# Scores a slot later, spreads at the slot's end, and two VectorE pairs merged, in a windowed-attention stack

## What is computed

```python
x = attn_layer(shift_tokens(x)) + x
x = ffn_layer(shift_tokens(x)) + x

def attn_layer(x):                       # 16 heads of 64
    q, k, v = split(x @ Wqkv)
    q, k = l2norm(q) * qs, l2norm(k) * ksc
    q = q * cos * scale + rotate_half(q) * sin * scale
    k = k * cos / scale + rotate_half(k) * sin / scale
    # local attention: windows of 32; a query sees itself and the 32 keys before it
    sim = where(mask, -max, 8 * q @ k.T)
    return softmax(sim) @ v @ Wo

def ffn_layer(x):
    a, gate = split(layernorm(x) @ W1 + b1)   # 2 x 341
    return a * gelu(gate) @ W2 + b2
```

## Time and profile before

| | before |
|---|---|
| median of 3 runs | 4340.56 us |
| profiled execution | 4352.9 us |
| its span, first to last instruction | 4351.2 us |
| TensorE busy | 4027.8 us (93%) |
| VectorE busy | 3345.6 us (77%) |
| ScalarE busy | 3100.0 us (71%) |
| GpSimd busy | 1798.7 us (41%) |
| mean granted TensorE clock | 0.959 of full speed |

### The profile page before, as it was taken

The page is one execution under the profiler, slowest core; times in us unless marked ns, Lnnn a source line. Parts: engine busy times, 40 slices in busy tenths (PEclk is TensorE's granted clock), DMA queues, the critical chain, the costliest instruction groups (busy, mean ns, idle before and its releaser), DMA issues. The chain is left out here.

```text
span 4351.2 us, 113662 instructions
## 1 busy us (share of the span) xinstructions
PE 4027.8 (93%) x43857; PEld 2388.8 (55%) x43857; DVE 3345.6 (77%) x4981; ACT 3100.0 (71%) x7032; POOL 1798.7 (41%) x1071
## 2 busy tenths in 40 slices
PE   7997999999999999999967689999999999999998
PEld 3443555555555555555536545555555555555554
DVE  5774888888888888888735478888888888888885
ACT  3555777777777777777762267777777778777776
POOL 3111444444444444444404534444444444444442
PEclk7997999999999999999986589999999999999999
DMA  2212444444443443444300044444434444444342
GB/s 44 31 21 70 95 111 102 99 101 101 105 111 90 111 107 90 111 99 103 84 10 3 3 107 109 101 97 109 110 87 115 102 100 100 102 105 111 92 100 52
DMA packets 232520, 380.78 MB, mean 88 GB/s; under 512 B 59364, under 2 KB 122336, under 8 KB 231688
## 3 DMA queue, kind: packets, MB, share of 16 engines
q1 hardware_dynamic: 231560, 372.20, 36.9%
q10 hardware_dynamic: 384, 0.79, 0.1%
HBM read 39.22 MB, written 1.05 MB: 9 GB/s over the span
## 5 line engine op out<-in xcount | busy, mean ns | idle before, releaser
L835 POOL TENSOR_TENSOR b_prob<-b_prob,b_rinv 128x768 f32<-128x768 f32 x384 | 564.3, 1469 | 1778.3 <-DVE b_rinv L1281 1778.3
L841 POOL TENSOR_TENSOR b_prc<-b_prc,b_sws 128x1024 f32<-128x1024 f32 x384 | 907.7, 2364 | 72.2 <-DMA b_sws<-b_prs 72.2
L1143 ACT ACTIVATE b_prob<-ps,b_nmx 128x96 f32<-128x96 f32 x3072 | 749.0, 363 | 0.0
L885 PEld LDWEIGHTS ps<-ident,b_prob 128*128 128x128 f32 x3072 | 367.9, 140 | 406.5 <-ACT b_pT L1079 232.8
L1216 DVE SCALAR_TENSOR_TENSOR b_prc<-ps,b_qks,b_rot 128x512 f32<-128x512 f32 x768 | 571.1, 744 | 14.0 <-ACT b_sq L1104 13.3
L1218 DVE SCALAR_TENSOR_TENSOR b_prs<-ps,b_qks,b_rot 128x512 f32<-128x512 f32 x768 | 570.1, 742 | 0.0
L885 PE MATMUL ps<-ident,b_prob 128*128 128x128 f32 x3072 | 513.0, 281 | 46.5 <-DVE b_kr L1264 37.1
L1262 DVE TENSOR_TENSOR b_prc<-b_prc,ps 128x512 f32<-128x512 f32 x384 | 263.6, 686 | 369.9 <-PE ps L950 288.3
L1079 ACT ACTIVATE b_pT<-ps 128x512 f32<-128x512 f32 x724 | 435.5, 601 | 154.1 <-PE ps L885 151.1
L987 PE MATMUL ps<-b_wqkv,b_xs 128*128 128x256 f32 x1536 | 435.0, 406 | 2.2 <-DVE b_prs L1218 2.2
L938 PE MATMUL ps<-b_xs,b_wqkv 128*128 128x512 f32 x768 | 408.9, 614 | 23.3 <-issue 10.0
(11 more groups left out here) (293 smaller groups left out, 7218.0 us busy)
## 6 DMA issues: line engine op xcount, KB each, us to landing
b_sws<-b_prs SPq DMA_DIRECT2D x1536, 128.0 KB, 2.3
b_vs<-b_va SPq DMA_DIRECT2D x384, 256.0 KB, 3.8
b_wqkv<-in_L_ffn_Wqkv SPq DMA_DIRECT2D x96, 192.0 KB, 3.6
b_xs<-y SPq DMA_DIRECT2D x126, 128.0 KB, 2.3
b_wo<-in_L_ffn_Wo SPq DMA_DIRECT2D x96, 64.0 KB, 3.1
b_xs<-y SPq DMA_DIRECT2D x42, 127.8 KB, 2.4
b_rot<-in_rot SPq DMA_DIRECT2D x2, 2048.0 KB, 7.8
b_w<-in_L_ffn_W SPq DMA_DIRECT2D x24, 170.5 KB
```

The costliest lines, as they stand in the source:

```text
L835: pool.tensor_tensor(prob[:, r, :, P - KEYS:P], prob[:, r, :, P - KEYS:P], rinv[:, r % 2, :].rearrange("p (b a) -> p b a", a=1).broadcast_ ...
L841: pool.tensor_tensor(prc[:, r, :, :], prc[:, r, :, :], sws[:, r % 2, :, :], ALU.add)\
L885: t = pe.transpose(bank[6][:, i * P:(i + 1) * P], prob[:, kd, 4 * e + 2 * h + m, :], ident[:, :])
L1143: g = act.activation(prob[:, kb, i, P - KEYS:P], wide[0][:, e * CH + m * KEYS:e * CH + (m + 1) * KEYS], ACT.Exp, bias=nmx[:, kb % 2, i:i + 1])
```

## The change

On TensorE, T0 now comes right behind Q, the scores follow it and are those of `c_` (unit(3)) instead of `b` (unit(2)), then K, T1, V, the strips, U, and at the end the spreads of b, just ahead of W. The spreads go to banks 7 and 6, the strips to bank 3, U and the feed-forward to bank 2. W, which writes bank 3 as before, waits in odd slots for `ln_done`, ScalarE's reading of the strips. On ScalarE the eight exponentials (now of `c_`) stand behind the copy of T1 and ahead of the copy of the values, `oT` and the inverse norms. On VectorE the maxima come behind the q product, then the split, the k product, the sums and reciprocals, and one normalising product at the end. The cosine and the sine product of q (and of k) are one instruction over 2 x 512 elements with the bank read twice, and so are the two normalising products, which read banks 6 and 7 in one call. The copy of T0 is always ScalarE's.

```diff
 # tensor
+                def spreads(b, d, pe=pe):
+                    UB, kb = um(b)
+                    pe.wait_ge(S["split_done"], ONE + twos(b) + 1)
+                    pe.wait_ge(S["kn_done"], ONE + UB)
+                    pe.matmul(bank[7], take[:, 2 * (kb % 2) + 1, :], rsp[:, :], start=True, stop=True)
+                    if d:
+                        pe.wait_ge(S["pt_cp"], ONE + 2 * um(d)[0] + 2)
+                    pe.matmul(bank[6], take[:, 2 * (kb % 2), :], rsp[:, :], start=True, stop=True).then_inc(S["nb_mm"], 1)
...
                         pe.matmul(bank[0][:, :], W[:, 0, :], X, start=True, stop=True).then_inc(S["q_mm"], 1)
...
-                    if d and before != 5:
-                        turn(UD, kd, 0)
+                        turn(UD, kd, 0, c_)
+                    if c_:
+                        UC, kc = um(c_)
+                        if not d:
+                            scores_ready(UC)
+                        mask(kc)
...
+                        g.then_inc(S["s_mm"], 1)
                     key_bank_free(f0)
                     if a:
                         pe.wait_ge(S["pk_done"], ONE + U)
                         pe.matmul(bank[1][:, :], W[:, 1, :], X, start=True, stop=True).then_inc(S["k_mm"], 1)
-                    if d and before == 5:
-                        turn(UD, kd, 1, b)
-                    if d and before != 5:
-                        turn(UD, kd, 1, b)
-                    if a and j % 2 and before != 5:
-                        strips(U, b)
-                    if b:
-                        if not d:
-                            scores_ready(UB)
-                        mask(kb)
...
-                        g.then_inc(S["s_mm"], 1)
-                    value_bank_free(f0)
                     if d:
-                        values(d, 0)
-                        values(d, 1)
+                        turn(UD, kd, 1)
...
                         m.then_inc(S["va_mm"], 1)
-                    if a and j % 2 and before == 5:
-                        strips(U, b)
+                    if a and j % 2:
+                        strips(U, d)
+                    value_bank_free(f0)
+                    if d:
+                        values(d, 0)
+                        values(d, 1)
+                    if b:
+                        spreads(b, d)
...
                         pe.wait_ge(S["o_cp"], ONE + UD + 1)
...
                         pe.wait_ge(S["y_add"], ONE + UD)
+                        if a and j % 2:
+                            pe.wait_ge(S["ln_done"], ONE + twos(a) + 1)
                         pe.matmul(bank[3][:, :], wo[:, pair(d), :], oT[:, kd % 2, :], start=True, stop=True).then_inc(S["wo_mm"], 1)
 # scalar
-                    if a and j % 2 and before != 5:
-                        inverse_norms(twos(a))
-                    if d:
-                        act.wait_ge(S["pv_mm"], ONE + 2 * UD + 2)
-                        act.activation(oT[:, kd % 2, :], bank[7], ACT.Copy).then_inc(S["o_cp"], 1)
...
                         act.preload_act_table_set("natural_log_exp_and_others")
+                    if c_:
+                        UC, kc = um(c_)
+                        act.wait_ge(S["smax_done"], ONE + UC + 1)
...
+                        g.then_inc(S["exp_done"], 1)
                     if a:
                         act.wait_ge(S["va_mm"], ONE + U + 1)
...
+                    if step == 2:
+                        act.wait_ge(S["f_norm"], ONE + C + 1)
+                        act.activation(fin, fin, ACT.Identity, bias=lng[:, 1:2]).then_inc(S["f_in"], 1)
+                    if d:
+                        act.wait_ge(S["pv_mm"], ONE + 2 * UD + 2)
+                        act.activation(oT[:, kd % 2, :], bank[2], ACT.Copy).then_inc(S["o_cp"], 1)
+                    if a and j % 2:
                         inverse_norms(twos(a))
 # vector
-                    dve.scalar_tensor_tensor(out=prc[:, r, i, :], in0=bank[i][:, :], scalar=scale,
-                                             in1=rot[:, 2 * i, t], op0=ALU.mult, op1=ALU.mult)
-                    dve.scalar_tensor_tensor(out=prs[:, r % 2, i, :], in0=bank[i][:, :], scalar=scale,
-                                             in1=rot[:, 2 * i + 1, t], op0=ALU.mult, op1=ALU.mult).then_inc(S[done], 1)
+                    both = bank[i][:, :].rearrange("p (a c) -> p a c", a=1).broadcast_to([P, 2, CH])
+                    dve.scalar_tensor_tensor(out=two_runs((2 * r + i) * CH, (8 + 2 * (r % 2) + i) * CH), in0=both, scalar=scale,
+                                             in1=rot[:, 2 * i:2 * i + 2, t], op0=ALU.mult, op1=ALU.mult).then_inc(S[done], 1)
...
-                        dve.tensor_copy(pT[:, 0, :, :], bank[6].rearrange("p (i q) -> p i q", i=4)).then_inc(S["pt_cp"], 1)
...
-                        dve.tensor_tensor(prc[:, kb, 0, :], prc[:, kb, 0, :], bank[2][:, :], ALU.mult).then_inc(S["qn_done"], 1)
-                        at = PAD + (kb % 2) * CH
-                        dve.tensor_tensor(kr[:, at:at + CH], prc[:, kb, 1, :], bank[3][:, :], ALU.mult).then_inc(S["kn_done"], 1)
...
+                        dve.wait_ge(S["s_mm"], ONE + UC + 1)
+                        dve.tensor_reduce(nmx[:, kc % 2, :], sc, AX.X, ALU.max, negate=True).then_inc(S["smax_done"], 1)
...
+                        at = 12 * CH + PAD + (kb % 2) * CH
+                        dve.tensor_tensor(two_runs(2 * kb * CH, at), prc[:, kb, :, :], norms, ALU.mult).then_inc(S["kn_done"], 1)
```

More of the change, by code:

```diff
@@ L624, in stack_semaphores, with stack @@
     return {n: sem("b_" + n) for n in names.split()}
-def stack(rep, ln_call, S, nc, w, c, bank, wide, xT, y, ident, identb, jmean, ln_eps, ss_eps, ss_back,
+def stack(rep, ln_call, S, nc, w, c, bank, wide, xT, y, ident, identb, jmean, norms, ln_eps, ss_eps, ss_back,
           ln_pe, ln_act, ln_dve, norm_done, cs, cen, sqr):
@@ L677, in stack, with two_runs @@
         ZERO = 8
+        def two_runs(first, second):
+            return bass.AP(roll[:, :].tensor, first, [roll[:, :].ap[0], [second - first, 2], [1, CH]])
         def um(u):
@@ L906, in values @@
                                 es = slice(e * DH, (e + 1) * DH)
-                                t = pe.matmul(bank[7][es, n * BLK:(n + 1) * BLK], v[:, es],
+                                t = pe.matmul(bank[2][es, n * BLK:(n + 1) * BLK], v[:, es],
                                               pT[:, h, 2 * e + m, o * BLK:(o + 1) * BLK],
@@ L1007, in slot @@
                             pe.wait_ge(S["ffw_ld"], ONE + 208 * (L0 + f[0] + 1))
-                        pe.matmul(bank[7], w1[:, 0, i * P:(i + 1) * P], fin, start=True, stop=True).then_inc(S["f_a"], 1)
+                        pe.matmul(bank[2], w1[:, 0, i * P:(i + 1) * P], fin, start=True, stop=True).then_inc(S["f_a"], 1)
                     if ok is not None:
@@ L1011, in slot @@
                         for i in range(FT):
-                            m = pe.matmul(bank[7], w2[:, i, :], hid[:, i, :], start=(i == 0), stop=(i == FT - 1))
+                            m = pe.matmul(bank[2], w2[:, i, :], hid[:, i, :], start=(i == 0), stop=(i == FT - 1))
                         m.then_inc(S["f_out"], 1)
@@ L1080, in turned, with query_squares @@
                             .then_inc(S["pt_cp"], 1)
+                    def query_squares():
+                        act.wait_ge(S["pq_done" if before == 5 else "q_mm"], ONE + U + 1)
+                        act.activation(sq[:, 2 * (r % 2), :], bank[0][:, :], ACT.Square).then_inc(S["sqq_done"], 1)
                     def inverse_norms(n):
@@ L1225, in slot @@
                     ok, OC = ffn_out(f0)
-                    follows = before in (0, 2, 4) or ok is not None
-                    if b and j % 2 == 0 and not follows:
-                        n = twos(b)
-                        dve.wait_ge(S["rn_done"], ONE + n + 1)
-                        dve.scalar_tensor_tensor(out=rsp[:, :], in0=rhi[:, :].bitcast(F32), scalar=minus_hi[:, 0:1], in1=rn[:, :],
-                                                 op0=ALU.mult, op1=ALU.add).then_inc(S["split_done"], 1)
                     if d:
@@ L1236, in slot @@
                         dve.tensor_tensor(ys, bank[3][:, :], ys, ALU.add).then_inc(S["y_add"], 1)
-                    if b and j % 2 == 0 and follows:
-                        n = twos(b)
-                        dve.wait_ge(S["rn_done"], ONE + n + 1)
-                        dve.scalar_tensor_tensor(out=rsp[:, :], in0=rhi[:, :].bitcast(F32), scalar=minus_hi[:, 0:1], in1=rn[:, :],
-                                                 op0=ALU.mult, op1=ALU.add).then_inc(S["split_done"], 1)
                     if before == 0:
@@ L1276, in slot @@
                         UC, kc = um(c_)
+                        sc = wide[0][:, :].rearrange("p (h c) -> p h c", h=2)[:, :, 0:4 * KEYS]\
+                            .rearrange("p h (i k) -> p h i k", k=KEYS)
+                        dve.wait_ge(S["s_mm"], ONE + UC + 1)
```

(10 more changed lines are left out.)

137 lines of the change are left out of this document (54 added, 83 removed).

## The result

The changed kernel takes **4742.95 us** (median of 4 runs, 4721.73 to 4753.18) against 4339.57 us for the kernel before in the same comparison: a ratio of **1.0915** (95% interval 1.0871 to 1.0959), 403 us slower. The forecast was 4583 us, slower by 242. The direction and the place are as forecast, the size is short, and the time lies above the range (4450 to 4690). The profiled execution took 4753.2 us (span 4751.4) against 4352.9 before.

A forecast was written before the change was run, and what follows sets the result against it. TensorE was taken to bound the kernel; waits ahead of W made slots 8.15 and 8.87 us, which with feed-forward terms gave 1882 us a stack against 1761, +242 for two: 4583 us against the median, range 4450 to 4690.

The forecast's parts named there:

- What bounds it: TensorE bounds the 192 slots of each stack, with 129 us a stack or 0.67 us a slot lost to waits.
- VectorE was the real limit: Rival, 8%: TensorE's stops vanish as VectorE's chain in a slot is cut in two; faster, 4210 us.
- The size of the stop: TensorE's new wait ahead of W, some 1 us in nearly every slot, some 390 us in all.
- The path to W: Even slot: W waits for ScalarE's copy to `oT`, starts at 7.21 us after a 1.15 us stop; slot 8.15.
- Odd slots: W also waits for Ln of the strips, starting at 7.93 us where TensorE came at 7.05; slot 8.87 us.
- Merging worth 0: VectorE's merged product takes 1.28 us; a faster one gains nothing, as the exponentials wait for T1's copy.
- half rate: Rival, 5%: VectorE's merged products take 2.35 us instead of 1.28, adding 232 us: 4815.
- Split: On VectorE behind the maxima, about 744 ns by the exclusion rule; 0 to 0.15 on the sums, nothing on W.
- the split meets GpSimd: Rival, 4%: the split waits for GpSimd's product and addition, delaying k's product and the sums; +96 us, 4680.
- Step 2 and table load: Feed-forward, 22 each a stack: step 2 delays W by 0.62 us, the table load ahead of the exponentials by 1.2.
- The terms with handovers I trust to 0.25 us a slot: Error allowed over 384 slots, giving the forecast's own range of 4485 to 4680 us.
- No change: Rival, 5%: ScalarE gets through 0.63 us a slot sooner than the rows say, so 242 shrinks to within 22 us.

The follow-up runs named there:

- a_unmerged: The changed kernel with both merged VectorE calls split up again, order, banks and layout kept: 4759.80 us, ratio 1.094.
- a_kfirst: The changed kernel with K issued ahead of the mask and the scores instead of behind them: 4713.97 us, ratio 1.0871.
- a_lnbank: The changed kernel with W written to bank 2, the feed-forward's a and out matmuls to bank 3, waiting for Ln in its place: 4618.05 us.
- a_halfexp: The changed kernel with every other one of a slot's eight exponentials left out: 4482.53 us, ratio 1.0298.
- a_best2: The changed kernel with W in bank 2, `oT` first, strips behind U, feed-forward matmuls ahead of W, K ahead of scores and mostly of T0: 4454.73 us.
- a_gate: The changed kernel with the feed-forward's mean, variance and gate matmuls ahead of W in steps 0, 1, 3 and 4: 4629.62 us.
- a_otfirst: The changed kernel with ScalarE's copy to `oT` ahead of the copy of the values in even slots: 4715.91 us, ratio 1.083.

## Why the prediction was right in kind and short in size

- **What bounds it: right.** TensorE's list, which is taken in order, sets the slot; VectorE's time does not (a_unmerged). *VectorE was the real limit* fell: TensorE stands still 394.6 us ahead of W, and shorter VectorE work changed nothing.
- **The size of the stop: right, but the number that agrees does so partly by luck.** The forecast counted a stop from the start that W would have had, for plain slots alone; the profile counts from the end of the matmul ahead, over all slots. Counted as the forecast did, from the starts (0.13 us behind the start of the second spread), the stops are 1.26 us in even slots (1.15 forecast), 0.88 in odd ones (0.88), 1.47 in step 2 and 2.22 with the table load, 481 us in all; the forecast's own terms, with those of step 2 and the table load, make 390 + 44 x (0.62 + 1.2) = 470.
- **The path to W: right in kind, each term a little short.** Forecast and measured, in an even slot, from Q's start: T1 3.11 and 3.30, its copy 3.80 and 3.99, exponentials 4.29 and 4.47, values 6.07 and 6.25, `oT` 6.56 and 6.72, W 7.21 and 7.50, next Q 8.15 and 8.44. Three things make it up. The mask follows T0 after 0.53 where I took 0.44, and T1 follows K, which stands behind the scores, after 0.96 where I took 0.86 (K's first matmul 697 ns, shown by a_kfirst); together 0.19 at T1. The copy to `oT`, close behind the exponentials, takes 0.68 where I took the 0.60 of the earlier trace rows, and the handover, in the median of the even slots, is 0.10 and not 0.05. W itself, behind a stop, needs 0.93 to 0.96 to the next Q where I took 0.86; the 0.08 for T0 that I had added does not occur in even slots.
- **Odd slots: right in kind.** W waits for Ln, which waits for `oT`, which waits for U (a_lnbank, a_halfexp). Measured 9.28 where 8.87 was forecast: T0 comes at 1.01 and not 0.86 (the late GpSimd product, for which 0.08 was allowed), the mask follows it after 0.57, T1 follows K after 0.96, and with that U starts at 5.88 (5.51 forecast) and W at 8.31 (7.93). The copy to `oT` (0.60) and Ln's handover (0.05) are as forecast here.
- **Merging worth 0: right here.** One product took 1283 ns, the forecast's 1.28, at full rate, so *half rate* fell. In the old order the merging is worth 0.7%, which the forecast didn't ask: it looked only at the new order.
- **Split: right.** It takes 744 ns in all 192 cases, beside no GpSimd operation, so *the split meets GpSimd* fell. By the exclusion that the Trainium skill (SBUF — State Buffer, "Who interferes with whom") states, a split with no GpSimd operation beside it should take what its shape needs; the trace agrees with 744 ns.
- **Step 2 and table load: right in kind**, 11.39 for 11.21 and 14.07 for 13.5. For step 2 the prediction's own starts give 8.65 - 7.93 = 0.72 and not the 0.62 that it put into the sum; the trace has 0.60 (W at 8.71 against 8.11 in the other odd slots with feed-forward matmuls), so the slip did no harm.
- **What the sum lacked.** The gap between 4583 and 4743 is 160 us. Set slot by slot against the forecast's terms for its kind, the 382 intervals are 141 us over; 16 lie around the stacks, where no change was forecast; the last 3 are rounding. The 141 are: 44 in even slots, 0.28 each (the three terms above); 28 in odd slots without the table load, 0.41 in plain ones and those with the mean, 0.2 in the others; 28 in slots with the table load, beyond the clock, where W starts at 9.65 for 9.17; 14 in the ten slots that begin a later layer, in one of which TensorE stops 1.5 us amid the scores (what ends that stop stays open); and 27 for 16 slots with the lower clock (last section).
- **The step that failed** is "The terms with handovers I trust to 0.25 us a slot". The mechanism was right and terms of the path to W were mis-sized, all to one side: plain slots took 0.28 and 0.41 us more than their sums, for the reasons given at *The path to W* and *Odd slots*. The terms had been taken from rows where each instruction stood behind another neighbour. The granted clock, at 27 us, was put at nothing without a reason; without it the time would have been about 4716, still above the range.
- *No change* fell, as the size of the stop shows.

What stays open: whether a version with the transposes a further slot later would take the loop of 8.6 us off the path (K ahead of T0, in a_best2, cut it to 7.86 in plain slots); it was not tried.

## What to carry to other kernels

An engine that works through its list in order wants, between an instruction and the one that needs its result after another engine's step, work that needs neither: before merging or shortening calls, ask what stands in the list ahead of the next waiting instruction, and what is queued on the other engine ahead of the step it waits for. When an order is changed, give the merged calls and the order two runs of their own: here the one gains 0.7% and the other loses 9%. And when the terms of a path are taken from rows, take them from rows with the same neighbour ahead, for behind a stop or another kind of matmul the same instruction took up to 0.1 us more here.

## What the runs showed of the hardware

- **The first matmul behind a change or a stop.** A pair of 128x512 matmuls takes 592 ns each in a dense run, 0.43 us apart. Behind the 64x96 scores (K), the first takes 697 ns and the second follows after 0.53; behind a stop (W), the first takes 667 or 697 ns and the second follows after 0.50 or 0.53.
- **The clock.** In 17 of the 44 slots with the table load (16 of them in the 382 intervals) TensorE's granted clock fell to half, 1.2 of 2.4 GHz, for 3.4 us. Each time TensorE had just stood still 1.95 to 2.05 us ahead of W, its longest stop in a slot. TensorE there, and the same line where the clock stayed (then two stretches of the first: us, busy us and instructions of PE, PEld, DVE, ACT and POOL, granted clock, DMA share, GB/s):

```profile
798.90 1.13 PE L1003 MATMUL ps<-b_oT,b_wo 128*128 128x512 f32 x2 [1.95 <-ACT b_rn L1091]
799.87 4.43 PE L1014 MATMUL ps<-b_hid,b_w 128*128 128x512 f32 x6
804.14 1.02 PE L1020 MATMUL ps<-b_xs,jmean 128*128 128x512 f32 x2
...
1301.22 2.74 PE L1014 MATMUL ps<-b_hid,b_w 128*128 128x512 f32 x6
```
```profile
796.00:801.00 5.00, 3.05 (x16) 1.46 (x13) 2.94 (x4) 4.30 (x11) 2.40 (x2) 0.91 0.01 3
801.00:805.00 4.00, 4.00 (x8) 1.58 (x7) 0.00 (x0) 0.00 (x0) 1.37 (x1) 0.68 0.33 77
```

  Where the lower clock lies over them alone, the six out matmuls take 4.43 us instead of 2.74, 1.69 more, and the slots without and with it differ by as much (14.07 and 15.75), so it cost 16 x 1.69 = 27 us in the intervals. In the slots with the table load the kernel before has none of these, nor has a_lnbank, whose W doesn't wait for Ln, nor a_halfexp; a_gate has 15, a_kfirst 21, a_unmerged 29 and a_otfirst 33. A stop can thus cost more than its length. Why it falls in some of these slots and not in others that look alike is not shown. The changed kernel's four executions took 4753, 4743, 4742 and 4722 us at a mean granted clock of 0.957, 0.959, 0.960 and 0.965.
- **A merged call over two far runs** of output and a bank read twice: 1277 to 1283 ns, the time of one plain 128x1024 call, against 2 x 744.
